# Breaking up a gate product and a projection between attention units in every second row

## The reference, cut to what matters

```
w = layernorm(x) + pos_emb
local = softmax(w w^T / 4) w            # 16 heads of 16 channels, windows of 128 tokens
comp  = conv(w, stride 4)               # 64 tokens
gt    = concat(comp, global_memory)     # 128 tokens, serve as keys and as values
glob  = softmax(w gt^T / 4) gt
mix   = sigmoid(concat(local, glob) @ gate_w + gate_b)
x     = x + (mix * local + (1 - mix) * glob) @ out_w + out_b
```

## Time and profile before

| what | value |
|---|---|
| median of three runs | 1112.37 us |
| profiled execution: time, span | 1110.8 us, 1109.0 us |
| PE busy over the span | 1060.6 us (96%) |
| PEld (weight load) busy | 914.7 us (82%) |
| DVE busy | 668.6 us (60%) |
| ACT busy | 646.8 us (58%) |
| POOL busy | 555.9 us (50%) |
| 60 to 420 us (rows 1 to 15): PE, DVE, ACT, POOL busy of 360 us | 342.93, 300.45, 229.07, 163.83 us |
| granted PE clock from 60 to 420 us | 1.00 |

### The profile page before, as it was taken

The page is one execution under the profiler, slowest core; times in us unless marked ns, Lnnn a source line. Parts: engine busy times, 40 slices in busy tenths (PEclk is TensorE's granted clock), DMA queues, the critical chain, the costliest instruction groups (busy, mean ns, idle before and its releaser), DMA issues.

```text
span 1109.0 us, 28590 instructions
## 1 busy us (share of the span) xinstructions
PE 1060.6 (96%) x11089; PEld 914.7 (82%) x11089; DVE 668.6 (60%) x1318; ACT 646.8 (58%) x873; POOL 555.9 (50%) x678
## 2 busy tenths in 40 slices
PE   7899999999999998999999998999999999999996
PEld 7777777777877776777778777899999999999995
DVE  4587888888888878788888887323424222222221
ACT  2456666565666666787777876454454444444441
POOL 6455355463535233433666566477744444444442
PEclk9999999999999999999999999999999999999998
DMA  8663644636454523666676568765432333233222
GB/s 215 170 185 105 169 125 112 171 93 170 112 142 124 144 82 76 175 171 175 143 162 173 143 173 261 202 110 57 45 55 44 53 48 49 49 48 49 48 44 24
DMA packets 174562, 130.22 MB, mean 117 GB/s; under 512 B 60810, under 2 KB 162927, under 8 KB 174432
## 3 DMA queue, kind: packets, MB, share of 16 engines
q1 hardware_dynamic: 155280, 106.79, 36.2%
q0 software_dynamic: 15840, 18.77, 11.8%
q10 hardware_dynamic: 3312, 2.85, 0.9%
HBM read 88.29 MB, written 40.08 MB: 116 GB/s over the span
## 4 chain that ended last, share of the span: by engine, by line
PE 55%; DVE 2%; ACT 1%; issue 1%; DMA 1%; POOLq 0%; ACTq 0%
PE ps_scores L1991 23%; PE ps_out L2026 11%; PE ps_turn L1854 5%; PE ps_misc L1886 3%; PE ps_out L1866 2%; PE ps_scores L1841 2%; PE ps_misc L1807 2%; PE ps_misc L1874 2%; PE ps_turn L1970 1%; PE ps_scores L1834 1%; PE ps_scores L1915 1%; PE ps_misc L1880 1%; PE ps_turn L1896 1%; ACT weights L2199 1%; DMA out<-y,out_row 1%
## 5 line engine op out<-in xcount | busy, mean ns | idle before, releaser
L1991 PEld LDWEIGHTS ps_scores<-xgT,weights 128*128 128x128 f32 x2240 | 260.3, 192 | 3.3
L1991 PE MATMUL ps_scores<-xgT,weights 128*128 128x128 f32 x2240 | 262.0, 275 | 0.0
L2508 DVE TENSOR_TENSOR gate<-ps_scores,silu 128x512 f32<-128x512 f32 x70 | 48.4, 691 | 237.5 <-ACT silu L2239 237.5
L960 ACT ACTIVATE weights<-ps_scores 128x1024 f32<-128x1024 f32 x128 | 126.8, 1023 | 76.8 <-PE ps_scores L632 61.3
L2239 ACT ACTIVATE silu<-ps_scores 128x512 f32<-128x512 f32 x70 | 41.8, 597 | 198.3 <-PE ps_scores L1991 198.2
L2026 PE MATMUL ps_out<-w2s,gate 128*128 x552 | 130.6, 379 | 0.0
L2232 ACT COPY weights<-weights 128x2048 f32 x68 | 129.9, 1910 | 0.2
L2026 PEld LDWEIGHTS ps_out<-w2s,gate 128*128 128x128 f32 x552 | 99.5, 190 | 10.7
L1133 DVE TENSOR_REDUCE sa_rowmax<-ps_turn 128x8 bf16<-128x1024 f32 x64 | 77.7, 1215 | 34.0 <-PE ps_turn L609 34.0
L965 ACT CAST weights<-ps_scores 8x1024 bf16<-8x1024 f32 x64 | 64.3, 1005 | 51.3 <-PE ps_scores L623 51.3
L1701 POOL DMA_INDIRECT xg<-xn_rows,slot_row x71 | 70.5, 993 | 25.1 <-issue 19.7
(11 more groups left out here) (332 smaller groups left out, 2123.4 us busy)
## 6 DMA issues: line engine op xcount, KB each, us to landing
weights<-w_scr SPq DMA_DIRECT2D x60, 256.0 KB, 3.9
weights<-q_scr SPq DMA_DIRECT2D x96, 128.0 KB
ks<-w_scr SPq DMA_DIRECT2D x24, 256.0 KB, 3.9
weights<-k_scr SPq DMA_DIRECT2D x48, 120.0 KB
w_scr<-wp SPq DMA_DIRECT2D x7, 768.0 KB, 3.9
q_scr<-qp SPq DMA_DIRECT2D x14, 384.0 KB, 3.6
weights<-in_w1T SPq DMA_DIRECT2D x10, 512.0 KB, 6.6
weights<-in_w3T SPq DMA_DIRECT2D x10, 512.0 KB, 8.6
```

What stands on the lines that cost most here:

```text
L960: act.activation(probs[s % 2][:], m.scores[s % 2][:], ACT.Exp, scale=SCALE).then_inc(exped, 1)
L1991: mm = pe.matmul(h_ps[r % 2][:, j, c, :], weights[:, j, k, c * P:(c + 1) * P], xgT[r % 2][:, k, :], start=(k == 0), stop=(k == DT - 1))
```

## The change

`gate` is taken apart into `gate_part`, which issues some of its four products, and `project` into `project_rows`, which issues the two products of one of the two token tiles. Four things move, in odd rows only:

- `turn_g` writes `side[1]`, a bank of `ps_turn`, and `copy_gT` reads it there (rows 1 to 13; the first, before the rows, stays in `ps_misc`).
- The wait on `gT_read` moves from the gate to `queries_scores(b, 3)`, which writes `ps_turn`.
- The four products of `gate(b - 1, 0)`: one goes behind `turn_g`, two stay, one goes behind `turn_max(b, 3)` (rows 1 to 13). ScalarE's tanh of them moves from in front of `copy_max(b, 3)` to behind it.
- The projection's first two products go behind `subtract_max(b, 6)`, the other two stay (rows 1 to 15).

```
-        def turn_g(p):
+        def turn_g(p, bank):
...
+        def gate_part(b, o, parts):
+            if b + o == 0 and parts[0] == 0:
                 pe.wait_ge(rest_in, N_REST)
+            for i in parts:
+                c = (0, 2, 1, 3)[i]
                 pe.wait_ge(att_read, OPR * b + OPR - (i < 2))
                 mm = pe.matmul(gate_place(b, o), gate_w[:, c, o * P:(o + 1) * P], attT[b % 2][:, c, :],
                                start=(i == 0), stop=(i == 2 * DT - 1))
+            if parts[-1] == 2 * DT - 1:
+                mm.then_inc(gate_made, 1)
...
+        def project_rows(b, n):
+            pe.wait_ge(mixed, b + 1)
+            for k in range(DT):
+                mm = pe.matmul(proj_place(b)[:, n * D:(n + 1) * D], mixT[:, k, n * P:(n + 1) * P], out_w[:, k, :],
+                               start=(k == 0), stop=(k == DT - 1))
+            if n == NT - 1:
+                mm.then_inc(proj_made, 1)
...
                 else:
-                    turn_g(p + 1)
+                    turn_g(p + 1, side[1])
+                    gate_part(b - 1, 0, range(1))
...
             values(b, 0)
             keys_scores(b, 1)
 
+            if nxt and not even:
+                pe.wait_ge(gT_read, p + 2)
             queries_scores(b, 3)
             subtract_max(b, 2)
             if old:
                 if (nxt or last) and even:
                     pe.wait_ge(wT_read, b + 3)
-                elif nxt:
-                    pe.wait_ge(gT_read, p + 2)
                 elif last:
                     pe.wait_ge(m.q_read, 2)
-                gate(b - 1, 0)
+                if nxt and not even:
+                    gate_part(b - 1, 0, range(1, 2 * DT - 1))
+                else:
+                    gate(b - 1, 0)
             values(b, 1)
 
             scores(b, 4)
             turn_max(b, 3)
             if (nxt or last) and even:
                 turn_w(b + 3, side[1])
+            elif nxt:
+                gate_part(b - 1, 0, range(2 * DT - 1, 2 * DT))
...
             subtract_max(b, 6)
             if nxt and even:
                 compress(p + 1, 1)
+            elif not even:
+                pe.wait_ge(tanh_done, DT * b)
+                project_rows(b - 1, 0)
             values(b, 5)
...
+                if even:
+                    project(b - 1)
                 else:
-                    pe.wait_ge(tanh_done, DT * b)
-                project(b - 1)
+                    project_rows(b - 1, 1)
...
             exponentials(b, 2)
-            if old:
+            if old and (even or not nxt):
                 squash(b - 1, 0)
 
             copy_max(b, 3)
             if (nxt or last) and even:
                 copy_wT(b + 3, side[1])
+            elif nxt:
+                squash(b - 1, 0)
```

More of the change, by code:

```diff
@@ L573, in cross_queries @@
             mm.then_inc(m.q_made, 1)
-        def turn_g(p):
+        def turn_g(p, bank):
             pe.wait_ge(conv_read, p + 1)
             for k in range(DT):
-                mm = pe.transpose(m.misc[:, k * P:(k + 1) * P], gn[:, k * P:(k + 1) * P], m.ident[:])
+                mm = pe.transpose(bank[:, k * P:(k + 1) * P], gn[:, k * P:(k + 1) * P], m.ident[:])
             mm.then_inc(gT_made, 1)
@@ L707, in turn_cross_row @@
             mm.then_inc(m.nT_made, 1)
-        def gate(b, o):
-            if b + o == 0:
+        def gate_part(b, o, parts):
+            if b + o == 0 and parts[0] == 0:
                 pe.wait_ge(rest_in, N_REST)
-            for i, c in enumerate((0, 2, 1, 3)):
+            for i in parts:
+                c = (0, 2, 1, 3)[i]
                 pe.wait_ge(att_read, OPR * b + OPR - (i < 2))
@@ L716, in gate @@
                                start=(i == 0), stop=(i == 2 * DT - 1))
-            mm.then_inc(gate_made, 1)
+            if parts[-1] == 2 * DT - 1:
+                mm.then_inc(gate_made, 1)
+        def gate(b, o):
+            gate_part(b, o, range(2 * DT))
+        def project_rows(b, n):
[5 more added lines that the diff above has]
+                mm.then_inc(proj_made, 1)
         def project(b):
-            pe.wait_ge(mixed, b + 1)
             for n in range(NT):
[L722 to L725, removed]
+                project_rows(b, n)
         def turn_c(c, bank):
@@ L763, in tensor_program @@
         turn_c(0, whole_out)
-        turn_g(0)
+        turn_g(0, m.misc)
         keep_warm(7)
@@ L916, in first_q, with copy_gT @@
             act.copy(wp[:, 0, :, r, :], wT[:, :, r, :]).then_inc(w_first, 1)
-        def copy_gT(p):
+        def copy_gT(p, bank):
             act.wait_ge(gT_made, p + 1)
@@ L922, in copy_gT @@
             act.copy(gT[:].rearrange("p k (x g) -> p k x g", g=G)[:, :, 0:3:2, :],
-                     m.misc[:, 0:DT * P].rearrange("p (k x g) -> p k x g", k=DT, g=G)).then_inc(gT_read, 1)
+                     bank[:, 0:DT * P].rearrange("p (k x g) -> p k x g", k=DT, g=G)).then_inc(gT_read, 1)
         def first_g(p):
@@ L1015, in scalar_program @@
         copy_cT(0, whole_out)
-        copy_gT(0)
+        copy_gT(0, m.misc)
         first_g(0)
@@ L1035, in scalar_program @@
             elif nxt:
-                copy_gT(b // R + 1)
+                copy_gT(b // R + 1, side[1])
             elif last:
```

## The result

The changed kernel takes 1110.37 us (median of 20 runs, 1106.41 to 1112.84), the kernel before 1114.39 us in the same number of runs: a ratio of 0.9966, 95% interval 0.9956 to 0.9976. By the ratio that is 3.8 us less (the two medians lie 4.0 us apart); 3.65 us were forecast, and 1108.7 us in a range of 1105.0 to 1113.5 us. The absolute time differs from the forecast mainly because the kernel before turned out at 1114.4 us where its first three runs gave 1112.4. The profiled execution of the changed kernel (1112.46 us, span 1110.7 us) is no faster than that of the kernel before: its row 1 begins 1.5 us later (62.62 instead of 61.10 us, at a granted clock of 0.97 instead of 1.00 up to there), the attention from there on is 1.3 us shorter, and what follows it is 1.5 us longer. The granted clock explains nothing of this last part: it is 1.00 there, 0.99 before the change.

The account below looks back on a forecast made before the run. PE was taken to bound the edited stage, with DVE beside it. Row 1: 0, row 3: 0.3, rows 5 to 13: 3.05, row 15: 0.3, together 3.65 us: 1112.37 - 3.65 = 1108.7 us, range 1105.0 to 1113.5.

Parts of the forecast that it names:

- First half: Odd rows, `turn_c` to `keys_scores(b, 3)`: moved gate products fill PE's waits; gain 0.61 us per row, not the 0.94 moved.
- the loop: `turn_max`, its copy on ACT, then `keys_scores`: 1.32 us long, which PE can't shorten, only fill.
- The cover of the second product by `attT`, 0.05 us: Row 9: the second gate product left in place starts at 260.68; DVE's `attT` is ready at 260.63.
- The moved wait on the gT copy: At `queries_scores(b, 3)`, start 259.31: ACT's copy ends at 259.11, so the wait is covered by 0.20 us.
- The race of L1116 and L449: DVE's scaling of w against GpSimd: DVE should win; rows 3 and 11 then win 0.78 instead of 0.61 us.
- Second half: Odd rows' end: the moved projection products gain 0 us, since `turn_c` waits for DVE's residual; row 15 gains 0.3 us.
- The tokens' DMAs: Six DMAs before `queries_scores(b + 1, 1)`: row 1 gains 0, row 3 0.3 us; in row 9 they fit.
- The rival "slower": Tokens' DMAs late in rows 3 to 13: 6 x 0.48 = 2.9 us lost, 1115.3 us; chance 0.12.
- The sum: Gains over the odd rows of the attention: together 3.65 us, 0.33%, giving 1108.7 us.

Follow-up runs that it names:

- the profile with unpaced `gs`: The changed kernel, with SyncE issuing the six DMAs of `gs` without waiting for earlier ones to land; ratio 0.9959 to the kernel before.

## Why the prediction was right, point by point

- **First half.** 0.56 to 0.57 us per odd row were measured (22.84 to 22.27 us), 0.61 forecast. What sets it is what the forecast named: the scores behind the gate's two products and the third maximum let `turn_max` start 264.64 - 257.90 = 6.74 us after `turn_c` (6.73 forecast). A piece costs more than the fourth part of the gate: 0.58 us where it stands alone behind `turn_max` instead of 0.47, and the two that stay take 1.12 instead of 0.94 us. That moved `values(b, 2)` by 0.05 us, but not `keys_scores`, which waits for ACT behind it (`values` needs 0.57 of the 0.68 us). The 0.05 us between 8.05 and 8.10 lie in the loop: `keys_scores` comes 1.36 us after `turn_max` instead of 1.32, with the copy on ACT 0.30 instead of 0.26 us behind `turn_max`.
- **The cover of the second product by `attT`, 0.05 us**, was too thin to call: the product stands in a group that took 1.12 us, and the trace names no wait in it. It costs nothing, because `turn_max` waits for DVE anyway.
- **The moved wait on the gT copy**: covered, as forecast.
- **The race of L1116 and L449**: won in every row from 3 on, as forecast. Rows 3 and 11 could so gain 0.78 us by the forecast, and row 11 gained 0.75 (23.02 to 22.27); the sum took only 0.61 for it. By the rule of the Trainium skill, "SBUF — State Buffer", section "Who interferes with whom", the one of DVE and GpSimd that issues first holds the shared ports for its whole instruction and the other blocks. The runs fit it in part: with L449 0.44 us behind, DVE's pair always takes 0.69 us. But at 0.37 us it takes 0.69 or 1.44, so that rows 9 and 11, which the forecast took as two cases that agree with the rule, have the same starts in the record and test nothing.
- **Second half: 0 us.** Right for rows 3 to 11, and shown from both sides: alone it gives nothing there, beside a shorter DVE chain it gives 0.64 us per pair. Row 13 was missed: the forecast says that the odd rows repeat row 9 within 0.2 us, but row 13 took 22.50 instead of 22.84 us before the change, its DVE chain is shorter, and it gains 0.19 us by this half alone. The last two rows gain 0.37 us where 0.3 was taken.
- **The tokens' DMAs.** The step that failed in size is "In row 9 it is there at 276.6, 0.7 us ahead": the cover was worked out for one row of one execution (273.8 + 2.8 us) and taken for all of the rows. `gs` was late in rows 3, 5, 7, 11 and 13 of the first profile after, and in four of these in the second. The rival "slower" named the mechanism; what it missed is that `turn_c` waits for the residual meanwhile, so that a delay up to about 0.8 us costs next to nothing and only the rest is paid: rows 3 and 5 lost 0.74 and 0.29 us of their gain. Row 13, where `turn_c` has less to wait for, lost 0.45 us, row 1 lost 0.89 us, and row 2 lost 1.15 us, nearly all by the lower clock (each against the profile with unpaced `gs`).
- **The sum** came out at 3.8 us against 3.65 by errors that offset, so that a miss of only 0.15 us is in part luck: row 11 and rows 3 and 13 were worth more on time (the profile with unpaced `gs` has a stage 5.0 us shorter than before), and the late `gs` took some of it back. The two profiles of the change show 1.3 and 1.9 us in the stage where the medians show 3.8 in all. Without the spells at half clock they would show about 2.4 and 3.1 us, an estimate from the 1.1 and 1.2 us above. What makes the rest of the difference was not settled: the kernel before was profiled in one execution only, one of its faster ones (1110.8 us against a median of 1114.39).

## What to carry to other kernels

Filling a gap of the busiest engine gains until the next engine's chain ends later. Before moving work, find the wait that the moved time will run into, and read whether the engine behind it is without a gap: if so the move gains nothing until that chain is shortened, and then both gains come together. A cover read from one execution held for the compute engines to some 0.05 us, but not for a race of two of them within a few hundredths of a microsecond, and not for DMAs: how late these land in row 11 changed by 1.1 us between two profiles of one program. Look at every row, too: one that is shorter than the others, as row 13, shows what happens when one instruction is missing.

## What the runs showed of the hardware that I had not expected

- A stall beside GpSimd that shows only as a long duration. DVE's product of two SBUF operands takes 0.42 us alone and 0.94 to 0.95 us when it starts while GpSimd's sum runs; the residual, one operand of which is in PSUM, takes 0.65 to 0.67 us in either case. In a list of waits it appears nowhere, and I counted it as work.
- What follows a long wait of PE. After 1.70 and 1.71 us without work in front of `gs`, PE's granted clock stood at 0.50 for about 3 us, and that cost 1.1 and 1.2 us on top of the wait.
- A product of 128x256 in f32 costs 0.47 us in a group of four and 0.58 us alone between bf16 groups; two take 1.01 us (275.16 - 274.15) in place of 0.94. `turn_g` and the three pieces take 0.75 + 1.12 + 0.58 = 2.45 us where `turn_g` and the whole gate took 0.31 + 1.88 = 2.19 us (a part of the 1.12 may be a wait for `attT`; the trace names none).
